# Software pipeline of a graph-attention edge pass: transposes of the weights and the weighted sums moved one visit later

## The reference, cut to what matters

```python
def _gatv2(x, src, dst, edge_attr, Wl, bl, Wr, br, We, att, bo):
    xl = x @ Wl.T + bl
    xr = x @ Wr.T + br
    m = xl[src] + xr[dst] + edge_attr @ We.T
    score = jnp.where(m > 0, m, 0.2 * m) @ att
    smax = jax.ops.segment_max(score, dst, num_segments=N)
    es = jnp.exp(score - smax[dst])
    denom = jax.ops.segment_sum(es, dst, num_segments=N)
    out = jax.ops.segment_sum((es / (denom[dst] + 1e-16))[:, None] * xl[src], dst, num_segments=N)
    return out + bo
```

## Time and profile before

| | |
|---|---|
| time of three runs | 7535.46 us median (7491.05 to 7591.95) |
| the profiled execution | 7500.06 us, its span 7498.2 us |
| mean granted TensorE clock | 0.875 of full speed |
| PE busy | 5710.3 us (76%) |
| PEld (weight loads) busy | 4119.1 us (55%) |
| DVE busy | 4066.2 us (54%) |
| POOL busy | 3271.5 us (44%) |
| ACT busy | 2555.9 us (34%) |
| HBM | 671.09 MB read, 88.81 MB written |

### The profile page before, as it was taken

How to read it: one execution, slowest core, us unless ns; L and a number is a source line. 1 busy time by engine, 2 the same in 40 slices (tenths; PEclk the granted TensorE clock), 3 DMA queues, 4 the chain that set the end, 5 groups by cost and what they waited for, 6 DMA issues and landing times. The chain is left out here.

```text
span 7498.2 us, 170900 instructions
## 1 busy us (share of the span) xinstructions
PE 5710.3 (76%) x40281; PEld 4119.1 (55%) x40282; DVE 4066.2 (54%) x12880; ACT 2555.9 (34%) x4880; POOL 3271.5 (44%) x3490
## 2 busy tenths in 40 slices
PE   4777767777777777477777777777777597999999
PEld 3555555555555555355555555555555593222589
DVE  6455555555555555545555555555555526888532
ACT  2333333333333333333333333333333204777410
POOL 3455555555555554255555555555555100333100
PEclk9888888888888888788888888888888797999999
DMA  3332323323333332333333333333333382222579
GB/s 77 75 76 68 80 68 79 81 70 79 79 73 77 79 72 70 65 73 82 83 70 80 76 74 79 73 80 79 71 80 81 114 328 74 107 107 107 214 302 376
DMA packets 689553, 764.70 MB, mean 102 GB/s; under 512 B 369221, under 2 KB 574252, under 8 KB 664371
## 3 DMA queue, kind: packets, MB, share of 16 engines
q1 hardware_dynamic: 561929, 577.69, 25.5%
q0 software_dynamic: 100352, 102.96, 7.4%
q10 hardware_dynamic: 27180, 82.93, 2.9%
HBM read 671.09 MB, written 88.81 MB: 101 GB/s over the span
## 5 line engine op out<-in xcount | busy, mean ns | idle before, releaser
L337 POOL DMA_INDIRECT gat_rows<-rows_scr,gat_idx x3136 | 3021.5, 964 | 2744.3 <-PE gat_aps L1353 1013.5
L1344 PE MATMUL gat_tps<-ident,gat_weights 128*128 128x128 f32 x3136 | 590.7, 318 | 1189.4 <-ACTq L1209 932.6
L1205 ACT ACTIVATE gat_weights<-gat_masked,gat_newtop 128x512 f32<-128x512 f32 x788 | 569.0, 722 | 1926.6 <-DVE gat_newtop L1125 1328.8
L1344 PEld LDWEIGHTS gat_tps<-ident,gat_weights 128*128 128x128 f32 x3136 | 377.0, 156 | 1369.4 <-ACTq L1209 1037.3
L1362 PE MATMUL gat_sps<-gat_relu,gat_att 128*128 128x256 f32 x3136 | 1063.6, 471 | 5.7 <-issue 5.7
L1125 DVE CUSTOM_DVE_ANT_0 gat_masked<-gat_sps,gat_miss,gat_oldtop 128x512 f32<-128x512 f32 x784 | 586.6, 748 | 733.7 <-remote 515.5
L1076 DVE TENSOR_SCALAR adj_hot_key<-adj_iota_key,adj_winbase,adj_key 128x392 bf16<-128x392 int16 x2416 | 963.9, 399 | 7.1 <-issue 7.1
L1353 PE MATMUL gat_aps<-gat_rows,gat_weightsT 128*128 128x65 f32 x6224 | 939.0, 303 | 0.0
L1353 PEld LDWEIGHTS gat_aps<-gat_rows,gat_weightsT 128*128 128x128 f32 x6224 | 920.5, 227 | 0.0
L1117 DVE COPY gat_oldtop<-gat_top 128x1 f32 x784 | 119.4, 152 | 1264.3 <-remote 587.5
L1075 DVE TENSOR_SCALAR adj_hot_lo<-adj_iota_lo,adj_low 128x128 bf16<-128x128 int16 x2416 | 628.3, 260 | 266.8 <-issue 112.3
(11 more groups left out here) (399 smaller groups left out, 7016.9 us busy)
## 6 DMA issues: line engine op xcount, KB each, us to landing
gcn_sum_adj<-adj_scr SPq DMA_DIRECT2D x98, 1568.0 KB, 8.4
gat_dstb<-dst_scr SPq DMA_DIRECT2D x784, 128.0 KB
gat_ea<-in_ea SPq DMA_DIRECT2D x784, 128.0 KB
gin_sum_adj<-adj_scr SPq DMA_DIRECT2D x49, 1568.0 KB, 8.5
adj_scr<-adj_tiles ACTq DMA_DIRECT2D x48, 1568.0 KB
at_adj<-adj_scr SPq DMA_DIRECT2D x60, 1024.0 KB, 9.5
gat_rows<-rows_scr,gat_idx POOLq DMA_INDIRECT x3136
gat_xr<-xr_scr SPq DMA_DIRECT2D x1568, 24.0 KB
```

Source lines behind the costliest of these rows:

```text
L337: pool.indirect_dma_start(ring.rows[:, u, c, 0:ROW], None, rows_d, bass.IndirectOffsetOnAxis(ap=ring.idx[:, u, c:c + 1], axis=0)).then_inc ...
L1205: act.activation(wts[:, j, :], masked[:, j, :], ACT.Exp, bias=newtop[:, j:j + 1], scale=-1.0)
L1344: last = pe.transpose(tps[:, c * P:(c + 1) * P], wts[:, j, c * P:(c + 1) * P], ident[:])
```

## The change

Nothing is computed differently. Four products are made later, and two engines order a step anew:

- T runs three visits behind (`turned` and `evac` get delay 3), A four behind (`sum` delay 4), the accumulator five behind (`acc` delay 5). `weight`, `top`, `score` and the masks stay where they were.
- TensorE's order in a step becomes A(u-4), M(u), T(u-3), S(u-1), C(u). A(u-4) needs `evac(u-4)` and `acc(u-5)`; T(u-3) needs `weight(u-3)` and `evac(u-4)`.
- ScalarE's order becomes fifth(u), evac(u-3), then weights(u-2) and shrink(u-2).
- VectorE waits for `sum(u-5)` before it adds it, and before `top(u-2)` it also waits for `weight(u-4)`.
- The drain gets a fifth step on VectorE (`CARRY = 5`) and a third on ScalarE; the registers that carry block numbers become five.

The diff, cut to its core:

```diff
-    delay = {"masked": 0, "message": 0, "fifth": 0, "relu": 1, "score": 1, "top": 2, "weight": 2, "turned": 2, "evac": 2,
-             "sum": 3, "acc": 4, "topped": 3, "olded": 2}
+    delay = {"masked": 0, "message": 0, "fifth": 0, "relu": 1, "score": 1, "top": 2, "weight": 2, "turned": 3, "evac": 3,
+             "sum": 4, "acc": 5, "topped": 3, "olded": 2}
...
 # vector, one step
-                    dve.wait_ge(s["sum"], count("sum", step, 4))
+                    dve.wait_ge(s["sum"], count("sum", step, 5))
...
                     dve.wait_ge(s["score"], count("score", step, 2))
+                    dve.wait_ge(s["weight"], count("weight", step, 4))
...
 # scalar, one step
             def visit(step, u, drained=False):
-                j = (u - 2) % 2
-                act.wait_ge(s["top"], count("top", step, 2))
-                act.wait_ge(s["turned"], count("turned", step, 4))
-                act.activation(wts[:, j, :], masked[:, j, :], ACT.Exp, bias=newtop[:, j:j + 1], scale=-1.0)
...
                     act.activation(relu[:, j, :], mps[j][:, 0:GE // 2], ACT.Copy, scale=0.2).then_inc(s["fifth"], 1)
 
-                j = (u - 2) % 2
-                act.wait_ge(s["turned"], count("turned", step, 2))
-                act.wait_ge(s["sum"], count("sum", step, 4))
+                j = (u - 3) % 2
+                act.wait_ge(s["turned"], count("turned", step, 3))
+                act.wait_ge(s["sum"], count("sum", step, 5))
                 act.activation(wtsT[:, j, :], tps[:], ACT.Copy).then_inc(s["evac"], 1)
+
+                if not drained or u < 2:
+                    j = (u - 2) % 2
+                    act.wait_ge(s["top"], count("top", step, 2))
+                    act.activation(wts[:, j, :], masked[:, j, :], ACT.Exp, bias=newtop[:, j:j + 1], scale=-1.0)
+                    act.wait_ge(s["acc"], count("acc", step, 6))
+                    act.activation(shrink[:, (u - 2) % 4:(u - 2) % 4 + 1], oldtop[:, (u - 2) % 4:(u - 2) % 4 + 1], ACT.Exp,
+                                   bias=newtop[:, j:j + 1], scale=-1.0)
+                    act.drain().then_inc(s["weight"], 1)
...
 # tensor, one step: the weighted sum now stands first
+                    j = (u - 4) % 2
+                    if not (first and u < 4):
+                        pe.wait_ge(s["evac"], count("evac", step, 4))
+                        pe.wait_ge(s["acc"], count("acc", step, 5))
+                        for c in range(GC):
+                            last = pe.matmul(aps[:, 0:D + 1], wtsT[:, j, c * P:(c + 1) * P],
+                                             rows[:, v, c, 0:D + 1].rearrange("p a f -> p (a f)"),
+                                             start=(c == 0), stop=(c == GC - 1))
+                        last.then_inc(s["sum"], 1)
...
-                    j = (u - 2) % 2
-                    pe.wait_ge(s["weight"], count("weight", step, 2))
-                    pe.wait_ge(s["evac"], count("evac", step, 3))
+                    j = (u - 3) % 2
+                    pe.wait_ge(s["weight"], count("weight", step, 3))
+                    pe.wait_ge(s["evac"], count("evac", step, 4))
                     for c in range(GC):
                         last = pe.transpose(tps[:, c * P:(c + 1) * P], wts[:, j, c * P:(c + 1) * P], ident[:])
                     last.then_inc(s["turned"], 1)
```

More of the change, by code:

```diff
@@ L1026, in _ @@
         def _(dve):
-            dve.sem_inc(s["sum"], FREE + 3)
+            dve.sem_inc(s["sum"], FREE + 4)
             dve.sem_inc(s["message"], FREE)
@@ L1173, in _ @@
                 turn(i + TAIL // TURN, False)
-            for u in range(DRAIN):
+            for u in range(CARRY):
                 drained(u)
@@ L1319, in visits @@
                     step = first_step + u
+                    j = (u - 4) % 2
+                    v = slice((slot + u - 4) % RING, (slot + u - 4) % RING + 1) if back is None or u >= 4 else bass.ds(back + u, 1)
+                    if not (first and u < 4):
[6 more added lines that the diff above has]
+                        last.then_inc(s["sum"], 1)
                     v, j = slot + u, u % 2
@@ L1345, in visits @@
                     last.then_inc(s["turned"], 1)
[L1347 to L1356, removed]
                     j = (u - 1) % 2
@@ L1372, in _ @@
             behind = pe.alloc_register(tag + "_pe_behind")
-            pe.reg_mov(behind, ODD - 3)
+            pe.reg_mov(behind, ODD - 4)
             with pe.Fori(0, tails) as i:
-                visits(i * TURN + TAIL, TURN, i + WOVEN, False, back=pe.snap(behind, min_val=ODD - 3, max_val=RING - 3),
+                visits(i * TURN + TAIL, TURN, i + WOVEN, False, back=pe.snap(behind, min_val=ODD - 4, max_val=RING - 4),
                        slot=ODD)
-                pe.reg_mov(behind, RING - 3)
+                pe.reg_mov(behind, RING - 4)
             for u in range(DRAIN):
                 step = tails * TURN + (TAIL + u)
+                j, v = (u - 4) % 2, ODD + u
+                pe.wait_ge(s["evac"], count("evac", step, 4))
+                pe.wait_ge(s["acc"], count("acc", step, 5))
+                for c in range(GC):
+                    last = pe.matmul(aps[:, 0:D + 1], wtsT[:, j, c * P:(c + 1) * P], rows[:, v, c, 0:D + 1],
+                                     start=(c == 0), stop=(c == GC - 1))
+                last.then_inc(s["sum"], 1)
+                if u < 3:
+                    j = (u - 3) % 2
+                    pe.wait_ge(s["weight"], count("weight", step, 3))
+                    pe.wait_ge(s["evac"], count("evac", step, 4))
+                    for c in range(GC):
+                        last = pe.transpose(tps[:, c * P:(c + 1) * P], wts[:, j, c * P:(c + 1) * P], ident[:])
+                    last.then_inc(s["turned"], 1)
                 if u == 0:
@@ L1388, in _ @@
                     last.then_inc(s["score"], 1)
[L1389 to L1403, removed]
                 count_edges(TAIL + u, counts[u % 2])
```

28 lines of the change are left out of this document (13 added, 15 removed).

## The result

| | before | after |
|---|---|---|
| median, us (4 runs each) | 7523.71 | 7854.48 |
| lowest to highest | 7491.05 to 7591.95 | 7825.18 to 7870.06 |
| profiled execution: time, span | 7500, 7498.2 | 7870.06, 7868.1 |

The ratio is 1.041, with an interval from 1.036 to 1.046: slower by 331 us, where I had forecast slower by 251 us.

A forecast was written before the change was run, and what follows sets the result against it. Bound: gather bursts holding PE's signals, 7.12 us a visit. 0.65 x 6.85 + 0.35 x 8.5 = 7.43 us; 784 x 0.31 = 243, plus 8 drain, +251 on 7500, plus 35 to the median: 7786 us; range 7650 to 8150.

The forecast's parts named there:

- What bounds the kernel: Edge passes, 784 visits of 7.12 us: no engine full; four-gather bursts and late PE signals set the pace.
- cycle of burst and held signal: Normal visit: sum seen, 0.7 us to first gather, held sums seen 5.9 us later; 6.6 to 6.8 us.
- Removed: the wait of T, worth 0: PE's wait for fresh weights before the transposes: taken as 0 in the normal visit, bounds 0 and 1.5 us.
- Moved: A to the head: TensorE's step: M, T, S, C queue behind A, which waits for ScalarE's copy after late `turned`; 6.85 us a visit.
- the rule for *when* it is seen: PE signals: 8 instructions issued since burst start pass, 22 or 23 are seen at 4.35 us, 32 at 5.8.
- Half clock: PE at 1.2 GHz after the wait: M slower, `turned` held to 5.8 us; 8.5 us in 35% of visits.
- ScalarE's new order, VectorE, GpSimd and SyncE: hidden: Other engines: ScalarE's reordering hidden by 1 us; VectorE's add 0, relu hidden; same gathers and loads, 0.
- Bursts of 8 become rare: Sign of being right, on GpSimd: two visits' gathers run together seldom; burst starts 6.85 and 8 to 9 us apart.
- Fast: Rival: `turned` passes with 22 issued, every visit takes the 6.6 us loop; -408 us, 7127 us; chance 0.33.
- Nothing: Rival: loop and mixture of starved visits stay; 7.1 us a visit, 7535 us; chance 0.15.
- all slow: Rival: nearly every visit held, idle PE bringing half clock; 8.5 us a visit, +1082, 8617 us; chance 0.12.
- bursts join for good: Extreme where sums come early enough for GpSimd's continuous gathers: 5.0 to 5.9 us a visit, whole 6540 us; no separate chance.

The follow-up runs named there:

- Burst after T: Changed kernel with one wait more: GpSimd starts a visit's gathers only after seeing `turned` of the same TensorE step as well as `sum`; 7378.88 us, ratio 0.975.
- A behind T: Changed kernel with TensorE's weighted sum A(u-4) put back behind the transposes T(u-3), all delays kept; 7649.15 us, ratio 1.013.
- its own kernel: Changed kernel with ScalarE's old order, weights and shrink of u-2 ahead of relu and the copy; 7899.32 us, ratio 1.046.

## Why the prediction was right, point by point

- *What bounds the kernel.* Right on the chip of the result: the cycle of burst and held signal. Burst after T shows the main part of it: an edit that only lets GpSimd start later, when T's signal has been seen, brings the ratio from 1.041 to 0.975, though it adds a wait and removes no work. That a burst by itself holds signals was an overreach of the rows: in the trace of the changed kernel on another chip bursts run without a gap and hold nothing, and the times of the kernel before on three chips (5832 to 5836 us) leave no room for held signals.
- *Removed: the wait of T, worth 0.* Right. It fell from 1189.4 to 1.1 us and gave nothing back. Its own worth, seen where nothing is held and the gathers are left out, is about 102 us, 0.14 us a visit, near the lower of the two ends that I kept (0 and 1.5). Most of the 1189 us was the holding seen at another place.
- *Moved: A to the head.* Right in kind. A behind T regains two thirds of the loss, and in the long intervals the next burst waits for a late A, as forecast. Its price holds too, counted from where `turned` is seen: copy, A and sum add 2.6 us (80 visits that see it at 4.35 us in the median take 6.95, 71 that see it at 5.91 take 8.58, forecast 6.85 and 8.5). What fails is the rule for *when* it is seen, by the instructions issued since the burst began. In the 121 visits with 24 to 27 issued the median is 4.45 us (forecast: 4.35, with 22 or 23), but a tenth lie below 2.9 and 39 at 5.5 or later.
- *Half clock.* Right number, wrong reason. The forecast took 35% of the visits as slow, with over 30 issued, so held to 5.8 us, so 8.5 us long, and all others as 6.85. By M's duration (over 1.7 us) 43% are slow. But with 36 to 39 issued, in 118 visits, `turned` is seen at a median of 4.33 us, at once in 36 of them, and at 5.5 us or later in 30. The 165 intervals with a slow M have a mean of 7.83 us and the 216 with a quick one 7.61: the price of the slow visits (8.5) was too high by 0.7 us, that of the others (6.85) too low by 0.8, and that 7.43 came near 7.58 is in good part luck. The order of cause is mostly the other way round: the interval *before* a slow M has a mean of 8.81 us, the one before a quick M 6.86. PE stands still in a long visit and comes back at half clock; half clock by itself adds little to the visit that follows. Why `turned` is held to 5.9 us in one visit and not in the next, at either clock, is not known.
- *The size.* 0.15 us a visit of difference (7.58 for 7.43) is 118 us. Of these the medians show 80 (331 against 251), since the profiled execution of the kernel before lay 24 us under its median and the one after 16 above.
- *ScalarE's new order, VectorE, GpSimd and SyncE: hidden.* For ScalarE's order shown by its own kernel (1.046 against 1.041). For VectorE not quite: the waits of the changed kernel between 500 and 5800 us have one that the forecast had at nothing, A's for the accumulator, beside the one forecast for the copy:

```profile
PE gat_aps L1331 <- ACT gat_weightsT L1215: 572.9, 185, 7.7
...
PE gat_aps L1331 <- DVE gat_acc L1120: 208.5, 118, 6.9
```

  Over 5300/7.58 = 699 visits that is 0.30 us a visit. What makes the add late was not tried.
- *Bursts of 8 become rare.* Half right: the joined bursts fall from 57 to 25 but don't vanish.
- *The rivals.* "Fast" fell: `turned` doesn't get through with 24 issued. "Nothing" and "all slow" fell by their times on this chip. The part of "fast" in which bursts join for good, priced at 5.0 to 5.9 us a visit, is what the other chips show: 5.0 in the trace of the changed kernel, and the same time in the kernel before. (The 6540 us put beside that price go with 5.85 us; at 5.0 the same sum gives 5873.)

What stays open: what holds the signals on the first chip and the one of the result. The gathers take part in the pattern, but nothing here shows how. One number points elsewhere too: the trace of the changed kernel holds 65,568 records of semaphore updates where signals are late and 122,863 on the chip where none is, for the same 170,431 instructions. Records are thus missing just where signals are held. Every run here has its span and clock from such a recording, so it isn't known whether the recording itself holds signals, or whether a kernel that nobody records would show the loss. Whether fewer gathers would free them there was not measured, as no such chip came up again. Nor was burst after T run on a chip that holds nothing; it may cost time there, since GpSimd is the bound and would have one more wait. And why bursts join at all in the kernel before was read from the rows, not tried.

## What to carry to other kernels

When a wait is removed from an in-order engine, look at what it will stand behind next: here the head of each step went to the one block whose input depends on a late signal, and all that the engine does in a step queued behind it. Put that block behind those whose inputs are ready, which here gave back two thirds of the loss, or start what goes with the delay only after the signal has been seen, which here gave back more than all of it. And take the size of a wait, and a lag of a signal, to a second chip before tuning by it: 1.7 ms of these 7.5 were there on one chip and not on the next.

## What the runs showed of the hardware that I had not expected

- The same program, instruction for instruction, takes 7560 us on one chip and 5832 to 5836 on three others. The traces of the changed kernel place the difference in the visits: after the last visit both take 1603 us more. It isn't in an instruction's duration at full clock: a gather takes 963 ns in the one and 964 ns in the other, the four matmuls of T 0.66 us in both. The mean granted clock differs (0.87 and 0.96); PE is busy 76% of the span in the one and 89% in the other.
- Where signals are held, the rows shown have them late by 1.5 to 7.6 us; in the trace from another chip T's is seen after 0.04 us and M's after 0.05, with GpSimd's gathers running without a gap in all of the 381 visits.
- A gather of 128 rows occupies GpSimd for 0.94 us and the next one follows 0.30 us later, so 1.25 us each, however many wait: four of them are a floor of 5.0 us under a visit, under which all of PE's work (4.33 us between two T in the median visit with half the gathers) is hidden.
